# Value products of two attention steps issued back to back on TensorE, in an adaptive-norm transformer layer on one core

## The reference, cut to what matters

```python
h = _layernorm(x, axis=-1) * (1 + ca) + sa
Q, K, V = split_heads(h @ W_q.T), split_heads(h @ W_k.T), split_heads(h @ W_v.T)
Q, K = _rope(Q, pos), _rope(K, pos)
score = jnp.einsum('bnqd,bnkd->bnqk', Q, K) / jnp.sqrt(jnp.float32(D_K))
score = jnp.where(causal[None, None], -jnp.inf, score)
attn = jax.nn.softmax(score, axis=-1)
out = jnp.einsum('bnqk,bnkd->bnqd', attn, V)
x = x + ga * (out @ W_o.T)
...
x = x + gb * _L0_ffn_ref(h, ...)
```

## Time and profile before

| | us |
|---|---|
| median of 3 runs | 951.28 |
| lowest and highest of them | 948.70, 952.42 |
| profiled execution, device time | 951.83 |
| profiled execution, span of the trace | 949.9 |
| TensorE busy in the span | 812.0 |
| VectorE busy in the span | 647.7 |
| ScalarE busy in the span | 506.2 |

### The profile page before, as it was taken

The page is one execution under the profiler, slowest core; times in us unless marked ns, Lnnn a source line. Parts: engine busy times, 40 slices in busy tenths (PEclk is TensorE's granted clock), DMA queues, the critical chain, the costliest instruction groups (busy, mean ns, idle before and its releaser), DMA issues.

```text
span 949.9 us, 20021 instructions
## 1 busy us (share of the span) xinstructions
PE 812.0 (85%) x5168; PEld 448.2 (47%) x5169; DVE 647.7 (68%) x1995; ACT 506.2 (53%) x944; POOL 317.2 (33%) x485
## 2 busy tenths in 40 slices
PE   3774488499999999999999999995887899999990
PEld 3432123133333333333333333355675797999980
DVE  7854897279887887899789988655758432333353
ACT  2342206166666665576567666777343365666660
POOL 9221201032211221112211122213372788755662
PEclk8887658599998999899899999998999999999995
DMA  6133419322211222023202220102031322211524
GB/s 192 42 106 94 117 37 200 80 52 52 52 34 19 51 51 48 4 51 51 52 16 36 51 52 2 33 1 54 26 101 34 102 79 76 76 60 59 151 89 138
DMA packets 61895, 62.23 MB, mean 66 GB/s; under 512 B 8896, under 2 KB 56640, under 8 KB 59520
## 3 DMA queue, kind: packets, MB, share of 16 engines
q1 hardware_dynamic: 57344, 51.80, 24.6%
q0 software_dynamic: 4480, 9.64, 2.8%
HBM read 37.48 MB, written 23.55 MB: 64 GB/s over the span
## 4 chain that ended last, share of the span: by engine, by line
PE 66%; DVE 10%; SPq 8%; issue 5%; DMA 5%; ACT 2%; POOL 1%; DVEq 1%; POOLq 0%; ACTq 0%
PE ps L1530 15%; PE ps L1477 15%; PE ps L1555 13%; PE ps L1710 8%; PE ps L1721 5%; SPq L477 3%; SPq L486 3%; PE ps L1731 2%; PE ps L1625 2%; PE ps L1617 2%; DMA k_parts_scratch<-qk_parts 2%; PE ps L1508 2%; DVE junk L1075 1%; DVE leftmax L1079 1%; DMA ka<-k_parts_scratch 1%
## 5 line engine op out<-in xcount | busy, mean ns | idle before, releaser
L811 ACT ACTIVATE probs<-ps 128x1024 f32<-128x1024 f32 (+3 forms) x384 | 299.0, 813 | 218.6 <-PE ps L1555 217.7
L1477 PE MATMUL ps<-ka,qa 72*128 72x512 bf16 (+3 forms) x768 | 230.1, 356 | 36.2 <-DMA ka<-k_parts_scratch 14.8
L1075 DVE CUSTOM_DVE_ANT_0 junk<-ps,tri 128x128 f32<-128x128 f32 (+3 forms) x512 | 222.5, 487 | 50.3 <-PE ps L1477 33.8
L662 POOL TENSOR_SCALAR_AFFINE_SELECT probs<-probs 128x512 f32<-128x512 f32 x128 | 81.1, 634 | 439.0 <-ACT probs L811 439.0
L1555 PE MATMUL ps<-qa,ka 75*128 75x512 bf16 (+3 forms) x768 | 195.6, 339 | 0.8 <-DMA qa<-mparts 0.6
L1530 PE MATMUL ps<-probs,v 128*32 128x512 f32 (+3 forms) x1536 | 171.1, 519 | 1.9 <-POOL probs L662 1.9
L1079 DVE TENSOR_REDUCE leftmax<-ps 128x1 f32<-128x512 f32 x256 | 162.5, 684 | 8.9 <-PE ps L1477 8.8
L1477 PEld LDWEIGHTS ps<-ka,qa 72*128 72x128 bf16 x768 | 68.2, 100 | 207.0 <-DVE rowmax L1075 81.8
L1555 PEld LDWEIGHTS ps<-qa,ka 75*128 75x128 bf16 x768 | 72.9, 101 | 82.8 <-ACT probs L811 33.8
L728 POOL DMA_INDIRECT routed_results_scratch<-y_s,s_dest x76 | 76.3, 1004 | 46.4 <-issue 40.3
L669 POOL DMA_INDIRECT slot_rows_scratch<-rows,slot x64 | 63.1, 986 | 57.5 <-DVE slot L1275 39.4
(11 more groups left out here) (184 smaller groups left out, 1051.1 us busy)
## 6 DMA issues: line engine op xcount, KB each, us to landing
qa<-q_parts_scratch SPq DMA_DIRECT2D x48, 192.0 KB
slot_rows_scratch<-cst SPq DMA_DIRECT2D x1, 5396.0 KB, 32.6
srow<-slot_rows_scratch SPq DMA_DIRECT2D x76, 71.0 KB
ka<-k_parts_scratch SPq DMA_DIRECT2D x32, 128.0 KB
q_parts_scratch<-qk_parts SPq DMA_DIRECT2D x24, 128.0 KB
k_parts_scratch<-qk_parts SPq DMA_DIRECT2D x24, 128.0 KB
ka<-k_parts_scratch SPq DMA_DIRECT2D x16, 192.0 KB
xs<-in_x SPq DMA_DIRECT2D x4, 512.0 KB, 6.8
```

The costliest lines, as they stand in the source:

```text
L662: nc.gpsimd.affine_select(out=p, in_=p, compare_op=ALU.is_ge, fill=0.0, base=0, pattern=[[0, HQ], [1, T]], channel_multiplier=-1).then_inc ...
L811: nc.scalar.activation(probs[s % 4][:, 2 * h:2 * h + 2, 0:CH - q0], ps[:, 2 * h:2 * h + 2, q0:CH], ACT.Exp, scale=SCALE).then_inc(s_exp, 1)
L1075: last = V.tensor_tensor_reduce(out=junk[:, bank - 5, at:at + w], in0=src, in1=tri[:, CH - w:CH], scale=1.0, scalar=LOW, op0=ALU.add, op1= ...
L1477: last = MM(ps[:, bank, at:at + w], qa[m][0:KR, h * S + q * T:h * S + (q + 1) * T], ka[m][0:KR, h * S + k0:h * S + k0 + w], start=True, st ...
```

## The change

The order on TensorE in `body` changes. In even steps no value product is issued. In odd steps two are issued back to back, of the steps s - 3 and s - 2, where before each step issued that of s - 2. In step 1 these are steps 10 and 11 of the quad before. All waits of the products, the ring's entries with their slots, and the programs of the other engines stay as they are.

```diff
                         if h % 2:
                             last.then_inc(s_scores, 1)
                             ring_entries(s * SLOTS + h // 2)
-                    if s >= 2:
-                        values_product(i, r, s - 2)
-                    elif not first:
-                        values_product(i, r - 1, NS - 2 + s)
+                    if s % 2:
+                        for back in (3, 2):
+                            if s >= back:
+                                values_product(i, r, s - back)
+                            elif not first:
+                                values_product(i, r - 1, NS + s - back)
                     ring_entries(s * SLOTS + 2)
```

## The result

The changed kernel takes 968.39 us (median of four runs, 965.07 to 973.25), beside 949.99 us for the kernel before on the same chip (four runs, 947.70 to 952.42). The ratio is 1.0197 with an interval of 1.0145 to 1.0250, so the merged products cost 18.4 us. The forecast was 969.0. The profiled execution of the changed kernel is its slowest, 973.25 us (span 971.3), 21.4 us above the profiled one of before; the accounts further down are made between these two.

A forecast was written before the change was run, and what follows sets the result against it. It took TensorE, VectorE and the three banks between them to bound a quad. 12.5 quads x 1.3 us less 1, plus 1.5 and 0.5 for quads 14 and 15, made 17.3 us more: 969.0 us, range 959 to 981.

The forecast's parts named there:

- What bounds a quad: In a full quad, TensorE and VectorE together set the time, with the three banks between them.
- The price of a pair: On TensorE, two merged products run without a seam and save 0.24 us, 1.4 us for six pairs a quad.
- The rival of the seamed pair: Within a pair, the second product's weight loads wait, costing up to 0.24 us more per pair; 988 us, chance 0.05.
- The rounds: Six rounds per quad, pair to pair; the larger of TensorE's and VectorE's work in each adds up to 28.1 us.
- the written-out order: One quad simulated bank by bank: 28.2 us before, 29.6 changed, pairs starting at 0, 5.3, 11.1, 17.4, 21.3 and 26.4.
- restarts: VectorE's wait behind wide pairs and ScalarE's hold on score banks: 0.3 to 0.4 us in four rounds, 1.2 to 1.6 together.
- The price of a quad: A full quad in the changed order takes 1.3 us more, between 0.9 and 1.7.
- ScalarE's hold on the scores: TensorE returns to a score bank that ScalarE still holds for 0.2 us, twice in a round.
- The two sums of rivals: Kernel times given for two rivals: 988 for pairs with a seam, 975 to 980 for one or two more half-clock stretches.
- The cold stretches: Some 27 us of quads 1 to 13 run at half clock behind passes' ends, gaining 1 us; further stretches thought unlikely.
- more half clock: Rival: longer waits cause further half-clock stretches, each of 10.2 us costing 5.1; one or two give 975 to 980, chance 0.12.
- The whole: Whole kernel 17.3 us slower: 15.3 for quads 1 to 13, 1.5 for quad 14, 0.5 for quad 15.

The follow-up runs named there:

- e1: Order of before with VectorE's row maxima taken over half of each piece's columns; 930.36 us, ratio 0.9812 to the kernel before.
- e11: Order of before with the sync engine's loads three steps later and a third list of ring slots that keeps the shift early; 935.07 us, ratio 0.9812.
- e2: Changed order with VectorE's row maxima taken over half of each piece's columns; 922.91 us, ratio 0.9740 to the kernel before.
- e12: Changed order with ScalarE's exponentials over half of the columns from quad 1 on, row maxima whole; 961.49 us, beside 952.97 for before.
- e5: Order of before with only the products of steps 4 and 5 merged, a wide pair; 961.32 us, ratio 1.0115 to the kernel before.
- e4: Changed order with row maxima over half the columns and, from quad 1 on, exponentials over half; 907.29 us, ratio 0.9594 to the kernel before.
- e8: Changed order with the ring's entries issued at other slots, from a list chosen for it; 976.35 us, ratio 1.0284 to the kernel before.
- e7: Order of before with the ring's entries of a full quad issued at other slots, from its own list; 950.79 us, ratio 0.9999.
- e9: Order of before with the sync engine's loads of the next sequence starting three steps later; 944.91 us, ratio 0.9925 to the kernel before.
- e10: Changed order with the sync engine's loads of the next sequence starting three steps later; 966.66 us, ratio 1.0146 to the kernel before.
- e3: Order of before with row maxima over half the columns and, from quad 1 on, exponentials over half; 930.55 us, ratio 0.9790.

## Why the prediction was right, step by step

**What bounds a quad: right.** TensorE, VectorE and the ring between them. e1 and e11 show that the order before is 0.7 to 0.9 us above TensorE's own work, e2 and e12 that some 70% of the changed order's extra hangs on VectorE's work and little on ScalarE's, e5 that half of it comes with one wide pair.

**The price of a pair: right.** The records of the pair of 512 and 512 columns reach over 1.92 us together (forecast 1.9), and one way out is gone between its halves. The rival of the seamed pair needed 2.1 us and falls. The rule of the Trainium skill in "TensorE: Matmul & The Clock Gate" (The mechanism), that a weight load overlaps with a running matmul only in another row group, does not hold for these column tiles; whether they are the section's other case, a load into the background weight buffer, no run shows. 1.92, 1.71 and 0.86 us leave no room for a seam, and in the pair at 503.93 the first eight weight loads are over by 504.08, while its first four matmuls run to 504.5 by their records:

```profile
503.92 0.16 PEld L1530 LDWEIGHTS ps<-probs,v 128*32 128x32 f32 x8 [0.23 <-issue]
```

**The rounds: right, and close.** The pairs start at 0, 5.34, 11.15, 17.63, 21.48 and 26.60 us behind that of steps 0 and 1 (516.14 and 521.48 in the fence above, then 527.29; the three earlier ones plus the quad's 29.84), where the written-out order had 0, 5.3, 11.1, 17.4, 21.3 and 26.4. The rounds last 5.34, 5.81, 6.48, 3.85, 5.12 and 3.24 us. Against the larger of the two engines' sums in the prediction that is +0.36, −0.05, +0.50, +0.38, +0.58 and −0.01: the extra is in the first, third, fourth and fifth round, those for which restarts were counted, and nowhere else. It adds up to 1.76, against 1.2 to 1.6.

**The price of a quad: a little small.** 1.51 to 1.77 us instead of 1.3, the spells below left aside, in eight quads of nine (1.06 in quad 13), within the 0.9 to 1.7 but for one kind of quad. The term that was too small is the restart behind a wide pair: VectorE stands there for 3.43 us in a quad, once for 1.64. What I named as its second half is not there: ScalarE's hold on the scores, "0.2 us, twice in a round", is worth 0.24 us of a whole quad (e12), and the scores wait for it less than before (1.2 us against 2.3). It would show only once VectorE were lighter (0.94 us from e2 to e4). The sum was near because one part was too small and the other too large: that is luck. The two sums of rivals, 988 and "975 to 980", are 1 us high (969 and 18 is 987, 969 and 5.1 or 10.2 is 974 to 979); nothing hangs on it.

**The cold stretches: the step that failed, though the errors cancelled.** The rival "more half clock" was set aside, with the expected waits called "well short of that". The half clock came all the same. Two of the four places in the changed kernel, the stretch ahead of each and the stretch at half clock, columns as above:

```profile
241.60:245.01 3.41, 2.63 (x15) 1.19 (x14) 3.30 (x12) 2.64 (x3) 0.63 (x1) 1.00 0.00 0
245.01:248.42 3.41, 3.41 (x16) 0.69 (x17) 2.50 (x12) 0.81 (x1) 0.63 (x1) 0.50 0.02 5
309.87:313.28 3.41, 2.63 (x16) 0.91 (x18) 3.12 (x15) 2.47 (x4) 0.63 (x1) 1.00 0.00 0
313.28:316.69 3.41, 3.41 (x18) 0.72 (x11) 1.71 (x8) 0.22 (x1) 0.63 (x1) 0.50 0.04 7
```

Around the shift (244.02 and 311.32), where TensorE waits 0.42 us for VectorE and then 0.34 for the bank behind it, it was busy 2.63 of 3.41 us, and the granted clock behind it is half of full, 1.2 instead of 2.4 GHz, for 3.4 us. The wide pair takes 3.29 us in it:

```profile
312.87 3.29 PE L1530 MATMUL ps<-probs,v 128*32 128x512 f32 x16
```

Four quads have such a spell, at some 1.6 us each (31.93 against 30.36, 31.49 against 29.84). The prediction had the 1.56 of 3.41 us of the earlier trace rows to go by and saw no fall behind anything fuller. But the waits around the shift don't settle it either. The quad at 502.38 has the same ones, and keeps the full clock:

```profile
501.01:504.42 3.41, 2.63 (x19) 0.94 (x21) 3.12 (x15) 2.47 (x4) 0.63 (x1) 1.00 0.00 0
```

So which quads get a spell is open.

**The whole: right by its sum.** Between the two profiled executions, +21.4 us: the nine quads away from the first and from the passes' ends +20.6, of which 6.4 are the four spells and 14.2 the ring (1.6 a quad); the three at the passes' ends −2.4, since VectorE's stop falls together with a wait there, and with some less half clock (10.2, none and 10.2, where it was 10.2, 10.2 and 6.8); the first −2.0 (half clock 4.1 instead of 8.6); quad 14 +1.6 (forecast 1.5); quad 15 +1.7 (forecast 0.5, it waits for ScalarE more often); the rest of the kernel +2.1 with one more spell, and −0.3 ahead of the shift at 183.15. The forecast had counted 15.3 for quads 1 to 13 and got 16.2, but by other terms: neither the +6.4 of the spells nor the −4.4 of the passes' ends and the first quad was in it, and that they nearly cancel is luck. The profiled execution is the slowest of the four; between the medians the change costs 18.4, and 17.3 was forecast.

**Where it failed further on.** In the experiments the quads at full clock came out as expected within 0.4 us (e8's in one of its two kinds), but for e7 and, by 0.3 to 1.0 us, e4. The times of whole kernels missed by some 9 us or more in e2, e4, e7, e8, e9 and e10, and by 6 to 8 in e1 and e3. In e2, e4 and e8 it was mostly the passes' ends, where a quad takes 28.3 us in e2 and 40.9 in e8; in e9 the stops there only shrank. The prediction has no term for VectorE's stop at the loop's branch, though the kernel before has it three times. The stop is in every run, and what changes from run to run is what it falls together with. Open is why it is twice as long in e8 (the packet of instructions starts 4.5 to 5.0 us behind the branch there and 0.9 to 1.8 in all other runs). No run took out the pass's end itself, by unrolling the loop.

## What to carry to other kernels

An engine that is busy 28.3 of 28.3 us need not be the bound: matmul records cover their latency, and weight loads that wait for a consumer show a full buffer. Before two long instructions that bypass a short ring are merged, compare their joined length with what the ring holds (1.9 us against three banks of 0.6 to 0.7 here), round by round: the larger of the two engines' work in each round adds up, and gains of one round don't pay for the next. Where such a ring costs time, try moving its entries in the program before saving the switches around it (e11 against e9, −9.8 us or 1.0%; but the list of e7 gave nothing). And an idle time that the profile puts down to a wait can be another stop underneath: compare the same place in a stretch where that stop can't be.

## What the runs showed of the hardware

- In the changed kernel TensorE fell to half clock for 3.4 us at a time within the quads, behind four stretches in which it was busy 2.63 of 3.41 us and stood for no longer than 0.42 us at once. Behind a fifth, as busy (501.01 to 504.42), it kept the full clock. In the earlier trace rows it fell for 10.2 us behind 1.56 of 3.41.
- At the branch back in the hardware loop VectorE stood for 2.7 to 4.4 us (7.2 to 7.6 in e8), in all 42 passes' ends of fourteen kernels, with one 8 KB packet of instructions inside each stop; ScalarE and GpSimd took 0.2 us. The profile shows it as idle time with no reason where the next bank has long been ready, and as a wait for TensorE where the bank comes within the last microsecond of it. In e8, whose quads are 1 us shorter elsewhere, a quad there took 40.9 us, where it takes 33.4 to 35.2 in the kernel before.
- Two products over the same four column tiles, back to back, run without a seam: 1.92 us for 512 and 512 columns, 0.86 for 256 and 128 (at full clock; 3.29 for the wide one at half clock).
